# Cross-attention and fp8 linear layer: scores taken relative to key 0 of each head, with 63 key columns a head

## The reference

```python
qp = layernorm(x) @ Wq.T
k, v = split(ctx @ Wkv_expand.T)
scores = einsum('bhqd,bhkd->bhqk', qh, kh) / sqrt(64)
scores = where(causal, scores, finfo.min)        # query q sees keys 0..q
attn = softmax(scores)
x = x + (attn @ vh, heads joined) @ Wout.T
x = x + fp8_linear(layernorm(x), weight)
```

## Time and profile before

| | us |
|---|---|
| median of 3 runs | 1798.99 (1798.11 to 1799.88) |
| the profiled execution's own time | 1799.89 |
| its span | 1798.1 |
| PE busy / DVE busy / ACT busy | 1744.1 / 1343.6 / 689.0 |

### The profile page before, as it was taken

How to read it: one execution, slowest core, us unless ns; L and a number is a source line. 1 busy time by engine, 2 the same in 40 slices (tenths; PEclk the granted TensorE clock), 3 DMA queues, 4 the chain that set the end, 5 groups by cost and what they waited for, 6 DMA issues and landing times.

```text
span 1798.1 us, 26754 instructions
## 1 busy us (share of the span) xinstructions
PE 1744.1 (97%) x10698; PEld 842.0 (47%) x10730; DVE 1343.6 (75%) x1844; ACT 689.0 (38%) x643; POOL 185.3 (10%) x143
## 2 busy tenths in 40 slices
PE   8689999999999999999999999999999999799998
PEld 4434454445444544454445444544454443455554
DVE  6776778677866787778777877787778665777776
ACT  5632133223322332233223322332233221788886
POOL 0000000000000000000000000000000011355555
PEclk9899999999999999999999999999999999899999
DMA  9664545454545354545454545454544444777763
GB/s 317 158 185 118 136 105 129 117 137 104 129 117 140 100 129 117 124 117 129 117 124 117 129 117 125 116 129 117 124 117 117 117 112 122 267 270 268 269 245 140
DMA packets 371689, 263.96 MB, mean 147 GB/s; under 512 B 322320, under 2 KB 324880, under 8 KB 371088
## 3 DMA queue, kind: packets, MB, share of 16 engines
q1 hardware_dynamic: 371600, 262.71, 53.7%
HBM read 119.28 MB, written 71.30 MB: 106 GB/s over the span
## 4 chain that ended last, share of the span: by engine, by line
PE 91%; issue 5%; DVE 2%; ACT 1%; DMA 1%; POOL 0%; SPq 0%; POOLq 0%; DVEq 0%
PE ps_all L623 70%; PE ps_all L760 12%; PE ps_all L610 2%; PE ps_all L632 2%; PE ps_all L596 1%; PE ps_all L597 1%; PE ps_all L693 1%; PE ps_all L575 1%; DVE n_buf L1066 1%; ACT tile_space L844 0%; ACT n_buf L832 0%; DMA tile_space<-tile_space 0%; DVE amax L1045 0%; DMA tile_space<-in_ctx_dram 0%; PE ps_all L565 0%
## 5 line engine op out<-in xcount | busy, mean ns | idle before, releaser
L623 PE MATMUL ps_all<-m_buf,tile_space 128*128 128x512 f16 x3072 | 681.6, 381 | 4.7 <-DVE wo_t L1267 4.7
L623 PE MATMUL ps_all<-n_buf,tile_space 128*128 128x512 f16 x3024 | 670.0, 379 | 0.0
L623 PEld LDWEIGHTS ps_all<-m_buf,tile_space 128*128 128x128 f16 x3072 | 298.5, 98 | 368.9 <-issue 13.1
L623 PEld LDWEIGHTS ps_all<-n_buf,tile_space 128*128 128x128 f16 x3024 | 292.1, 98 | 350.1 <-issue 6.2
L760 PE MATMUL ps_all<-wo_t,tile_space 128*128 128x512 bf16 x992 | 231.1, 381 | 2.8 <-DVE tile_space L1377 1.2
L858 ACT ACTIVATE tile_space<-tile_space,neg_mean 128x1024 f32<-128x1024 f32 x63 | 72.4, 1149 | 327.6 <-DVE neg_mean L1153 327.6
L514 POOL TENSOR_TENSOR rstd_x<-veps_x,minus_half 128x1 f32<-128x1 f32 x64 | 35.3, 551 | 1388.2 <-DVE veps_x L1096 1388.2
L854 ACT ACTIVATE tile_space<-tile_space,score_scale 128x1024 f32<-128x1024 f32 x64 | 73.5, 1148 | 230.9 <-DVE tile_space L1123 230.9
L760 PEld LDWEIGHTS ps_all<-wo_t,tile_space 128*128 128x128 bf16 x1024 | 97.8, 98 | 107.7 <-issue 1.7
L850 ACT ACTIVATE tile_space<-tile_space 128x1024 f16<-128x1024 f32 x64 | 67.6, 1057 | 184.5 <-DVE tile_space L1133 184.5
L1083 DVE SCALAR_TENSOR_TENSOR tile_space<-tile_space 128x1024 f16<-128x1024 f32 x64 | 78.4, 1225 | 64.0 <-ACT tile_space L850 64.0
(11 more groups left out here) (128 smaller groups left out, 1700.6 us busy)
## 6 DMA issues: line engine op xcount, KB each, us to landing
tile_space<-in_x_dram SPq DMA_DIRECT2D x128, 512.0 KB, 3.8
x_scratch<-tile_space SPq DMA_DIRECT2D x64, 512.0 KB, 3.0
m_buf<-x_scratch SPq DMA_DIRECT2D x32, 512.0 KB, 4.0
tile_space<-x_scratch SPq DMA_DIRECT2D x32, 512.0 KB, 4.0
out_dram<-m_buf SPq DMA_DIRECT2D x32, 512.0 KB, 2.9
out_dram<-tile_space SPq DMA_DIRECT2D x31, 512.0 KB, 2.9
m_buf<-in_L_xattn_Wq_dram SPq DMA_DIRECT2D x4, 1024.0 KB, 11.1
n_buf<-in_L_xattn_Wout_dram SPq DMA_DIRECT2D x2, 2048.0 KB, 18.3
```

The source lines that it names most:

```text
L623: mm = nc.tensor.matmul(to[:, cols], left[:, ls, c * P:(c + 1) * P], right[:, rs, c, cols], start=(c == 0 and i == 0), stop=(c == CT - 1 a ...
```

## The change

Every key's context is replaced by its difference from the context of key 0 of the same batch (`ctx_d`, one VectorE instruction), and the keys are expanded from the differences; the values still come from `ctx_t`. So column 0 of each head of M is zero. It is no longer stored: `m_buf` holds 63 columns a head, 1008 of its 1024 columns, packed. The score product is a function of its own (`scores`), with 504 columns a matmul: eight heads of 63, which are written to PSUM as eight runs of 63 columns, each one column past the head's start. Column 0 of each head in `ps_s` is set to zero once, in the setup, by VectorE, and stays so. `take_m` reads 63 of 64 columns of each head and writes them packed. `make_m` and everything behind the scores are as before. Two semaphores are new: `ctx_made` (TensorE waits for the differences before the first key expansion) and `zero_made` (TensorE waits for the zeros before the first S).

```diff
+    REST = SK - 1
+    RH = NH // 2 * REST
-        ctx_t = tile_space[:, 3, :].rearrange("p (a k) -> p a k", a=LT)
+        ctx_t, ctx_d = (tile_space[:, i, :].rearrange("p (a k) -> p a k", a=LT) for i in (3, 2))
...
+        def rest_of(to):
+            return to.rearrange("p (h k) -> p h k", k=SK)[:, :, 1:SK]
+
+        def keys_of(s, c):
+            return m_buf[:, s, c, 0:NH * REST].rearrange("p (h k) -> p h k", k=REST)
...
             def expand(g2):
+                if g2 == 0:
+                    pe.wait_ge(ctx_made, 1)
+                of = ctx_d if g2 < QUAD else ctx_t
...
-                                              wkv_t[:, lt, g * P:(g + 1) * P], ctx_t[:, lt, :],
+                                              wkv_t[:, lt, g * P:(g + 1) * P], of[:, lt, :],
...
+            def scores(left, weave=lambda c: None, ready=lambda c: None):
+                for c in range(CT):
+                    ready(c)
+                    for i, (ls, rs) in enumerate(PASSES):
+                        for half in range(2):
+                            mm = nc.tensor.matmul(rest_of(ps_s[:, half * HALF:(half + 1) * HALF]),
+                                                  left[:, ls, c * P:(c + 1) * P],
+                                                  m_buf[:, rs, c, half * RH:(half + 1) * RH],
+                                                  start=(c == 0 and i == 0),
+                                                  stop=(c == CT - 1 and i == len(PASSES) - 1))
+                    if c == CT - 1:
+                        mm.then_inc(s_full, 1)
+                    weave(c + 1)
...
-                    split_product(ps_s, xt_buf[1 - e], m_buf, s_full, between, m_chunk)
+                    scores(xt_buf[1 - e], between, m_chunk)
...
-            split_product(ps_s, xt_buf[0], m_buf, s_full)
+            pe.wait_ge(zero_made, 1)
+            scores(xt_buf[0])
...
-                nc.scalar.activation(m_buf[:, 0, c, :], grow_ps[c % 2][:], ACT.Copy,
+                nc.scalar.activation(keys_of(0, c), rest_of(grow_ps[c % 2][:]), ACT.Copy,
...
+            dve.wait_ge(turned_read, 1)
+            by_batch = lambda t: t.rearrange("p a (b k) -> p (a b) k", k=SK)
+            nc.vector.tensor_tensor(by_batch(ctx_d), by_batch(ctx_t),
+                                    by_batch(ctx_t)[:, :, 0:1].to_broadcast([P, LT * B, SK]),
+                                    ALU.subtract).then_inc(ctx_made, 1)
             for i in range(4):
                 dve.wait_ge(got_wq[i], 16)
...
-                nc.vector.scalar_tensor_tensor(out=m_buf[:, 1, c, :], in0=grow_ps[c % 2][:], scalar=M_SCALE,
-                                               in1=m_buf[:, 0, c, :], op0=ALU.mult,
+                nc.vector.scalar_tensor_tensor(out=keys_of(1, c), in0=rest_of(grow_ps[c % 2][:]), scalar=M_SCALE,
+                                               in1=keys_of(0, c), op0=ALU.mult,
...
             for c in range(CT):
                 take_m(c, c // 2)
                 take_wout(c)
+                if c == CT - 2:
+                    dve.wait_ge(wt_free, CT - 1)
+                    nc.vector.memset(heads(ps_s[:])[:, :, 0:1], 0.0).then_inc(zero_made, 1)
```

More of the change, by code:

```diff
@@ L187, in xattn_ffn_kernel @@
         turned_read = sem("turned_read")
+        ctx_made = sem("ctx_made")
+        zero_made = sem("zero_made")
         wt_full = sem("wt_full")
```

## The result

| | before | after |
|---|---|---|
| median, us | 1798.99 (1798.11 to 1799.89, 5 runs) | 1808.06 (1807.56 to 1809.49, 5 runs) |
| ratio | | 1.0052, 95% interval 1.0037 to 1.0067 |
| span of the profiled execution, us | 1798.1 | 1805.8 |

The change made the kernel 9.1 us slower, where 9.7 us faster was forecast. The chain that ended last still lies on PE for 91%, so no wait took over. First the groups by line of the kernel after, which answer to the earlier trace rows; L635 is the score product, L650 the output product, L1105 and L865 the takes of M on VectorE and ScalarE.

The account below looks back on a forecast made before the run. TensorE was taken to bound the kernel: -9.65 us from 2898 score matmuls, 0 from taking M and 0 from the setup, so 1798.99 - 9.65 = 1789.3 us. Recorded range 1787.8 to 1840 us; the forecast's own 1787.8 to 1794.

Parts of the forecast that it names:

- The bound: Whole kernel: TensorE bounds it, with 91% of the chain; 2898 of 3072 score matmuls on the path, saving 9.65 us.
- The column's price: Score matmuls: 0.4165 ns a column plus 2.7 ns fixed; eight columns less save 3.33 ns a matmul.
- Where the columns go in PSUM: Score output in eight runs of 63, odd starts: gaps taken as free, 212.6 ns a matmul; upper bound 231.5 ns.
- The second: Score output: each new run costs TensorE time like a new matmul, up to +15.5 ns; 1799 to 1846 us; chance 0.12.
- The first: Score output: pairs can't span heads or odd starts, so 63 columns take 32 slots; gain zero, 1799.0 us; chance 0.14.
- The third: Score output: odd starts split pairs, half the columns at half rate, +105 ns a matmul, 2106 us; chance 0.17.
- The rule of the Trainium skill: PSUM writes: 8-byte lines, two f32; any non-contiguous pattern slows matmuls significantly, making the sum zero or positive; no price given.
- Taking M: M's copies from PSUM on VectorE and ScalarE: 19 and 16 ns shorter each, effect on the total 0 us.
- The setup: Before the first S: differences of 1.22 us and zeros of 0.2 to 0.3 us, both covered, effect 0.
- The wait before the last pair of N: Step 0 of each batch: TensorE's 0.34 us wait absorbs what 18 matmuls save, growing to 0.40 us.

Follow-up runs that it names:

- one even run: Against the changed kernel, each score matmul's 504 columns are written to PSUM as one run from the bank's start: 1790.1 us, ratio to before 0.9947.
- the ordering by key: Against the changed kernel, scores and M ordered key first, head second, zero columns together, matmuls of 496 and 512 columns; computes the reference: 1789.3 us, ratio 0.9946.
- 8 x 62, even: Against the changed kernel, each score matmul writes eight runs of 62 columns (496), each from column 2 of its head: 1780.0 us, ratio 0.9892.

## Why the prediction was wrong

- *The bound.* Right: PE in the order of its program, 2898 matmuls on the path. 2898 x 3.33 ns gives 9.65 us for the loss (9.1 measured between the medians), and with one even run the same the other way (8.9 measured, 9.6 in the ordering by key).
- *The column's price.* Right: 0.4165 ns from 512 and 64 columns gives 212.5 and 209.2 ns, both measured where starts and lengths are even.
- *Where the columns go in PSUM.* This is the step that failed. I took the lower of two bounds, 212.6 ns (upper 231.5), on the ground that the rows show a cost of columns and a constant; but all rows had even starts and even lengths, so they couldn't speak. The cost of the odd runs was put at zero without a row that held the pattern. The runs showed 219.2 ns, that is 6.7 ns (eight pairs) over the column count and 3.3 ns over the 215.8 of before. That turned 9.65 us of gain into as much loss.
- *The rivals.* The second was nearest in its time (1799 to 1846 us), but not in its mechanism: breaks as such are free (8 x 62, even). That the recorded range, 1787.8 to 1840 us, holds the measured 1808.1 is thus luck: it reached there for a mechanism that the runs refute. The first came nearest in its mechanism, pairs that can't straddle, but had too small a size: it gave 32 slots for a run of 63, in all the 4 extra pairs that would only cancel the gain, where 8 were measured. At the lower level its count is exact (427 ns, as for 512 columns). The third, half rate for half the columns, would cost 105 ns a matmul; 6.7 were paid.
- *The rule of the Trainium skill.* "PSUM — Partial Sum Buffer", Specifications, says any non-contiguous pattern slows matmuls significantly. The runs agree with it in that a pair of f32 columns (8 bytes) is the unit of the cost, and refute "any": eight gaps of two columns cost nothing, and the worst pattern here costs 6.7 of 219.2 ns.
- *Taking M.* 1203 and 1005 ns against 1201 and 1002 forecast: right, and hidden.
- *The setup.* Right: the differences ran at 8.06 for 1.23 us, before the reduction that had to wait for its data until 10.45, and the zeros took 0.07 us beside the last take of M; the first expansion began at 11.49 and the first S at 79.32.
```profile
8.06 1.23 DVE L1057 TENSOR_TENSOR tile_space<-tile_space 128x1024 f32<-128x1024 f32 x1 [8.06 <-ACT tile_space L815]
10.45 2.29 DVE L1062 TENSOR_REDUCE small<-m_buf 128x1 f32<-128x2048 f32 x1 [1.17 <-DMA m_buf<-in_L_xattn_Wq_dram]
...
76.83 0.07 DVE L1314 MEMSET ps_all<- 128x16 f32 x1
```
- *The wait before the last pair of N.* It was to absorb what 18 matmuls a batch save; here they lost time, and the wait shrank by it. The waits of PE for VectorE's takes of N, in us, times, longest:
```profile
PE ps_all L623 <- DVE n_buf L1099: 5.1, 9, 1.8
```
Two of the nine lie in the first batch (1.37 and 1.78), so the other seven are (5.1 - 3.15) / 7 = 0.28 us each, 0.06 less than before: 18 x 3.3 ns. Right.

## What to carry to other kernels

Where TensorE bounds the kernel, fewer columns save their full count, 0.42 ns each here at the upper clock level, if every run of the output in PSUM starts on an even column and has an even length. A single run with an odd start loses only one pair of it; many odd runs can lose more than the columns save. A layout that drops one column of each group should be turned round so that the dropped columns lie together (here: key first, head second) rather than leave odd runs. And where an edit brings a pattern that no row of the trace has, the rows' regularity is no evidence for its price: the nearest rows bound it, they don't choose within the bounds.

## What the runs showed of the hardware

- At the upper clock level an odd start costs a matmul one pair of columns (0.83 ns) a run, whatever the run's even length (504, 126 or 62 columns); gaps of two columns between even runs cost nothing.
- Odd lengths cost even with even starts: 2, 3 and 5 pairs for 2, 4 and 8 runs.
- At the lower level (granted clock 0.50) the cost is the pairs touched and no more: 427 ns for eight runs of 63 with odd or even start, as for 512 columns.
- VectorE read f32 scores from PSUM at a stride of 16 columns at the same 1222 to 1225 ns for 1024 elements as head by head, and took M at a stride of 64 columns in 1203 ns for 1008, as head by head.
